# Four graph layers on one core: the edge half of the edge network moved into layer 1, products in PSUM, and a narrower layer 0

## What is computed

```python
x = _layernorm(x + _L0_gnn_ref(...))   # per type and head: softmax over the edges of a destination, weighted sum of x[src] @ W[type]
x = _layernorm(x + _L1_gnn_ref(...))   # three graph attention layers one after the other, 4 heads of 32
x = _layernorm(x + _L2_gnn_ref(...))   # an edge network, then a node network
x = _layernorm(x + _L3_gnn_ref(...))   # sum over the out-edges, one matrix, relu
```

```python
h = jnp.concatenate([x[row], edge_attr], axis=1)   # 128 + 128 columns
h = jax.nn.relu(h @ w1a + b1a)                     # 256 columns
h = jax.nn.relu(h @ w1b + b1b)                     # 256 columns
h = h @ w1c + b1c
summed = jax.ops.segment_sum(h, col, num_segments=n)
```

## Time and profile before

| what | us |
|---|---|
| median of 3 runs (10702.52 to 10762.04) | 10716.57 |
| the profiled execution | 10696.98 |
| its span, first to last instruction | 10695.3 |
| layer 0, 430 to 1885 | 1455 |
| layer 1, 1991 to 6545 | 4554 |
| edge network, 6605 to 8680 | 2075 |
| layer 3 scatter, 8900 to 10600 | 1700 |

### The profile page before, as it was taken

One profiled execution on the slowest core, in us unless ns is written; L12 is line 12 of the kernel. 1 busy time (PEld: TensorE's weight loads), 2 busy tenths in 40 slices (PEclk: granted clock), 3 DMA queues, 4 the chain that ended last, 5 costly groups with the idle time before them and its releaser, 6 DMA issues. The chain is left out here.

```text
span 10695.3 us, 86620 instructions
## 1 busy us (share of the span) xinstructions
PE 4520.8 (42%) x16860; PEld 2720.4 (25%) x16860; DVE 5556.2 (52%) x10266; ACT 2086.2 (20%) x4254; POOL 7165.4 (67%) x5805
## 2 busy tenths in 40 slices
PE   6388887211111200001000003888888885433332
PEld 5133333211110200001000001444444443333332
DVE  6399998644444344443444444555565544444443
ACT  1211111211111211112111112333333331000002
POOL 2466666488887688886888884555555526888885
PEclk8688888555555555555555556999999985555555
DMA  2433334322223222223222223333333313444445
GB/s 67 122 59 59 59 59 54 87 42 42 42 41 39 45 42 42 42 43 44 43 42 43 42 42 73 90 87 87 88 93 85 89 32 31 36 36 36 36 36 95
DMA packets 775295, 608.14 MB, mean 57 GB/s; under 512 B 441381, under 2 KB 661028, under 8 KB 774068
## 3 DMA queue, kind: packets, MB, share of 16 engines
q0 software_dynamic: 325728, 497.67, 26.0%
q1 hardware_dynamic: 449492, 109.67, 4.9%
HBM read 479.64 MB, written 127.21 MB: 57 GB/s over the span
## 5 line engine op out<-in xcount | busy, mean ns | idle before, releaser
L1640 POOL DMA_INDIRECT big<-table_layer,idx_L x2688 | 3528.8, 1313 | 952.3 <-issue 818.9
L2311 POOL DMA_INDIRECT sums_by_source<-msg,to x896 | 1420.4, 1585 | 286.9 <-issue 241.2
L1651 PE MATMUL own_ps_L<-of_tile_L,big 50*128 50x4 f32 x1344 | 313.1, 354 | 2694.4 <-DVE of_tile_L L1700 2694.4
L936 POOL DMA_INDIRECT big<-table_layer,idx_L x912 | 948.7, 1040 | 517.3 <-issue 299.0
L1710 DVE TENSOR_TENSOR z_L<-own_ps_L,big 128x64 f32<-128x64 f32 x168 | 43.9, 261 | 2034.5 <-DMA big<-table_layer,idx_L 2034.5
L1861 POOL DMA_INDIRECT big<-table_layer,from x900 | 861.1, 957 | 274.3 <-issue 274.3
L1651 PEld LDWEIGHTS own_ps_L<-of_tile_L,big 50*128 50x128 f32 x1344 | 298.6, 325 | 2712.2 <-DVE of_tile_L L1700 2704.7
L1911 PE MATMUL ps<-big,w 128*128 128x512 f32 x1792 | 829.6, 606 | 0.0
L1740 DVE TENSOR_TENSOR_SCAN big<-h 128x2244 f32<-128x2244 f32 x168 | 811.9, 4833 | 15.2
L999 PE MATMUL sums_L<-h,ident 128*128 128x512 f32 x1344 | 723.1, 688 | 169.6 <-issue 132.9
L1998 DVE TENSOR_REDUCE partial<-big 128x128 f32<-128x512 f32 x448 | 462.1, 1041 | 552.0 <-ACT big L1945 494.7
(11 more groups left out here) (411 smaller groups left out, 8962.7 us busy)
## 6 DMA issues: line engine op xcount, KB each, us to landing
big<-table_layer,idx_L POOLq DMA_INDIRECT x3600
table_layer<-xr SPq DMA_DIRECT2D x49, 298.0 KB
big<-table_layer,from POOLq DMA_INDIRECT x900
sums_by_source<-msg,to POOLq DMA_INDIRECT x896
sums_by_source<-big SPq DMA_DIRECT2D x4, 3200.0 KB
q<-sums_by_source SPq DMA_DIRECT2D x28, 448.0 KB, 6.2
own_L<-own_parts_layer SPq DMA_DIRECT2D x232, 40.0 KB
table_layer<-st_L SPq DMA_DIRECT2D x98, 66.0 KB
```

Source lines behind the costliest of these rows:

```text
L936: G.indirect_dma_start(out=g[b][:, u, s, :], out_offset=None, in_=table, in_offset=bass.IndirectOffsetOnAxis(ap=at, axis=0)).then_inc(gath ...
L1640: G.indirect_dma_start(out=ring[b][:, s, :], out_offset=None, in_=tab1_d[l], in_offset=bass.IndirectOffsetOnAxis(ap=idx[b][:, s:s + 1].bit ...
L1651: last = PE.matmul(own_ps[b % 2][:, c * B:(c + 1) * B], own1T[:, c * P:(c + 1) * P], of_tile[b % 2][:, :], start=True, stop=True)
L2311: G.indirect_dma_start(out=sum_d[s], out_offset=bass.IndirectOffsetOnAxis(ap=to[u][:, s:s + 1], axis=0), in_=msg[u][:, s, :], in_offset=No ...
```

## The change

Three things are changed, and small ones that they need.

1. **Layer 0.** `weigh` is one instruction of 2048 elements an item in place of four of 512. The weights (`wt`) lie in PSUM, two banks. The own part is picked by one copy and three predicated copies on a mask of the slot's type. The item sums use four PSUM banks in place of eight.
2. **Layer 1.** The products, the weights and the carried-in column lie in PSUM (`prod_ps`), handled in two halves of two heads: copy, copy, two products, scan of 1122 elements, twice a batch. The shrink factors stay in SBUF. In the first 13 turns of each of the three (52 of 56 batches), PE, ACT and SP also work through 5 or 6 chunks of 128 edges per batch: SP loads them in order, PE transposes them and multiplies by `w1a`'s edge half, ACT copies both results, SP stores 256 columns an edge to a new DRAM tensor `he_d`. Over the three layers this covers all edges. PE's small matmuls for a batch now stand one batch earlier.
3. **Edge network.** POOL gathers the window of four finished rows from `he_d` (4 KB a partition) and the four source rows. DVE adds the two in SBUF (1024 elements), PE transposes the sum (8), ACT applies the relu straight from PSUM, PE multiplies the second layer only. The edge transposes, the edge matmul, the mask and DVE's two copies and two additions are gone. Empty slots point at a source row lowered by 1e31, so that their first relu is 0; what they then add to the sums is a constant, taken off in the node network through a third row of `deg_d` and `brow`.

The core of the diff:

```diff
-                NB = 2 * B if T > 1 else B
+                NB = B
                 banks = [pb(f"sums_{tag}{v}", [P, 512], fp32, ph) for v in range(NB)]
...
-                        A.activation(sc[b][:, :, :, :], sc[b][:, :, :, :], ACT.Exp).then_inc(weighed, 1)
+                        A.activation(wt[b][:, :, :, :], sc[b][:, :, :, :], ACT.Exp).then_inc(weighed, 1)
...
-                            for u in range(B):
-                                V.tensor_tensor(zt[:, u, :, :].rearrange("p s (t w) -> p s t w", t=T),
...
+                            V.tensor_scalar(is_type[:, :, :], mask[b][:, :, :], 0.0, None, ALU.is_equal)
+                            V.tensor_copy(z[:, :, :, :], bc(ob[b][:, :, 0:ZW], 2, S))
                             dve.drain()
-
-                            V.tensor_reduce(z[:, :, :, :].rearrange("p u s w -> p (u s) w"),
...
+                            for t in range(1, T):
+                                V.copy_predicated(z[:, :, :, :].rearrange("p u s w -> p (u s) w"),
+                                                  bc(is_type[:, :, t], 2, ZW),
+                                                  bc(ob[b][:, :, t * ZW:(t + 1) * ZW], 2, S))
+                                dve.drain()
...
+                            last = V.tensor_tensor(
+                                prod[PROD[u]][:, :, :].rearrange("p s (t h c) -> p s t h c", t=T, h=H),
+                                bc(w.rearrange("p s (t h) -> p s t h", t=T), 4, C),
+                                bc(g[b][:, u, :, 0:D].rearrange("p s (h c) -> p s h c", h=H), 2, T), ALU.mult)
...
+                    prod_ps = pb(f"products_{tag}", [P, 3 * 512], fp32, ph)
+                    prod = prod_ps[:, 0:WIDE // 2].rearrange("p (a s) -> p a s", s=SLOTS + 1)
+                    wt = prod_ps[:, 1472:1472 + H * SLOTS].rearrange("p (h s) -> p h s", h=H)
...
+                            for f in range(2):
+                                rows = slice(f * half * (C + 1), (f + 1) * half * (C + 1))
+                                V.tensor_copy(prod[:, :, 0], tot[1 - b % 2][:, rows, SLOTS])
+                                V.tensor_copy(p4[:, :, C, 1:SLOTS + 1], wt[:, f * half:(f + 1) * half, :])
+                                for c in range(half):
+                                    hd = f * half + c
+                                    last = V.tensor_tensor(p4[:, c, 0:C, 1:SLOTS + 1], bc(wt[:, hd, :], 1, C),
...
+                        def hidden(i, b):
+                            k = i * NB + b
+                            for v in range(2):
+                                m = min(CHUNKS[b] - 4 * v, 4) * P
+                                act.wait_ge(e_turned, k * 2 + v + 5)
+                                A.activation(eT[:, 4 * v * P:4 * v * P + m], psE[:, 0:m], ACT.Copy).then_inc(eT_ok, 1)
...
+                        pool.wait_ge(joined, g + U - NH + 1)
...
+                        G.indirect_dma_start(out=gh[u % NH][:, :, :].rearrange("p s c -> p (s c)"), out_offset=None,
+                                             in_=he_flat, in_offset=bass.IndirectOffsetOnAxis(
...
+                        V.tensor_tensor(x_, x_, flat(gh[u % NH][:, :, :]), ALU.add).then_inc(joined, 1)
```

343 lines of the change are left out of this document (193 added, 150 removed).

## The result

The changed kernel took **10828.21 us** in the median of 5 runs (10809.93 to 10857.98), the kernel before 10716.57 beside it (5 runs too, in the range given above for 3): a ratio of 1.0112, 95% interval 1.0094 to 1.013. It is slower by 1.1%. I had forecast 9470 us, with 0.96 for faster and a range of 9190 to 9860. The forecast was wrong, by 1358 us and in its sign.

What follows compares the result with a forecast made beforehand. It took POOL's gather issue to bound layer 1, DVE layer 0 and PE the edge network. 10697 - 924 (layer 1) - 493 (edge network) + 171 (layer 0) + 10 (small things) = 9461, forecast 9470 us, range 9190 to 9860.

Steps and rivals of the forecast that it cites:

- What bounds layer 1: Layer 1: POOL's gather issue sets the pace; three gathers blocked beside DVE's products and scan cost 5.6 us a batch.
- The inference on the Trainium skill's page "SBUF — State Buffer": Layer 1 rival: gathers stay blocked, as descriptor generation is not stalled by tensor_tensor; nothing saved, 10385 us, chance 0.05.
- So the edge work is priced at nothing. Its cover is POOL's 20 us of gathers: Layer 1: edge work on PE, ACT and SP fits under POOL's gathers, ACT done at 19 to 21.5 us; cost nothing.
- the term of -924 us: Layer 1: with the gathers unblocked a batch falls from 26.1 to 20.6 us, saving 924 us over 168 batches.
- Another bound in layer 1: Layer 1 rival: ACT, with PE's edge work ahead of its keeps, bounds a batch at 22.3 us; 9750 us, chance 0.11.
- I subtracted 6.8 from 8.99: Edge network: POOL becomes the bound, an item falls from 8.99 to 6.8 us, saving 493 us over 225 items.
- the price of the new addition: Edge network: DVE's addition reads both inputs from SBUF and costs POOL's gathers 0.35 us an item.
- the mechanism: Layer 0: PE's fourth item waits for its bank, pauses 5.8 us, runs at half clock; DVE waits about 6 us.
- The predicated copies: Layer 0, DVE: three of 320 elements at 0.42 us each, 1.3 us in all; at twice that, 2.5.
- my 171: Layer 0: a batch grows from 24.9 to 27.9 us, losing 171 us over 57 batches.
- PSUM does not slow DVE: Layer 1 rival judged here: strided products and scan in PSUM slow DVE, kernel slower than before, 10771 us, chance 0.03.
- the rival said: Edge network rival: PE pauses, falls to half clock and needs about 8.3 us an item; 9799 us, chance 0.12.

Runs made afterwards that it cites:

- change_third: The changed kernel, unedited, on another chip: 9277.89 us, 0.908 of the kernel before.
- psum_products_alone: The kernel before with only layer 1's products and weights in PSUM, products and scan in two halves: 10275.08 us, 0.968 of the kernel before.
- twelve_small_third: psum_products_alone with 12 more semaphore increments on ACT per batch of layer 1: 9287.51 us, 0.909 of the kernel before.
- psum_alone_again: psum_products_alone, unedited, run once more on another chip: 10421.74 us, 0.973 of the kernel before.
- groups 1 and 3: Follow-up runs on two chips, each beside the kernel before, which took 10611.53 and 10712.04 us there.
- groups 2, 4 and 5: Follow-up runs on two other chips (the last two sets on the same one), beside the kernel before at 10235.79, 10222.68 and 10216.61 us.
- change_l0_keep_first: The changed kernel with ACT's first keep of a layer 0 batch put before the next batch's exponentials: 8942.01 us, 0.8752 of the kernel before.
- gathers_paced: psum_products_alone with a memset and a drain on POOL behind every second gather of layer 1: 12402.2 us, 1.212 of the kernel before.

## Why the prediction was wrong

**What bounds layer 1: right.** POOL's issue set the pace and three gathers a batch were blocked by DVE's products and scan. With PSUM operands a gather takes 0.952 us in the median; 18 of 2688 take over 1.4 us and none over 1.73, where 364 took over 1.4 and 178 over 3. Where nothing else intervenes the batch is 20.3 us (forecast 20.6). The inference on the Trainium skill's page "SBUF — State Buffer" (Who interferes with whom), that `tensor_tensor` with both inputs in SBUF does not stall descriptor generation, is contradicted: beside such products two gathers took 1.31 and 1.65 us, and with one operand of products and scans in PSUM POOL's gathers lost 954 us, most of it beside the scans.

**"So the edge work is priced at nothing. Its cover is POOL's 20 us of gathers": the step that failed, under one condition.** The overlap was wrong, and with it the 20.6 us a batch. The cover was the free time of ACT and SP under POOL's 20 us. In change_third the cover holds. In the run of the record it doesn't, and two parts of the loss can be told apart. The first has nothing to do with the edge work: once POOL is unblocked, on the chips with phases, ACT and SP don't keep up even with the `keep`s and index fetches that the kernel before had. psum_products_alone stands at 23.8 to 24.5 us a batch in its two runs, over 3 us above the forecast. The second is the edge work, 2.6 to 2.7 us more in the second and third tries and 4.5 to 5.3 in the first. POOL waits 1113 us more for indices than in change_third, and layer 1 takes 1148 us more (4495 for 3347). So the term of -924 us became +196. That it is ACT and SP that are late, and that the same code is not late on another chip, is shown; what makes them late stays open. My rival "Another bound in layer 1" named ACT with edge work ahead of the `keep`s, but at 22.3 us a batch it was too small, and it held the cause to be the amount of work.

**The edge network: the base was mis-sized.** I subtracted 6.8 from 8.99. But 8.99 held lost time already: the same code runs at 7.13 us an item in the groups without phases, bound there by PE, as a window over this stage in twelve_small_third shows (columns as in the earlier trace rows):

```profile
5620.00:7216.00 1596.00, 1581.49 (x7002) 872.79 (x7003) 1143.83 (x1965) 674.70 (x1094) 1068.16 (x1119) 1.00 0.44 112
```

PE is busy 1581 of 1596 us at full clock, where it was 1744 of 2075 at 0.92 in the record. Without phases the gain is 7.13 - 6.56 = 0.57 us, 128 us in all, not 493; with phases it was 8.99 - 8.15, 180 us from first to last start. The trace had told it: I read the mean of 225 starts and never asked why the median was 8.50 and some steps 19. What was right is the price of the new addition. Beside it five gathers take 0.37 us more an item (means of 1.029 and 1.031 us for 0.957 and 0.953; 0.26 without phases), forecast 0.35.

**Layer 0: the mechanism was right.** PE's pause was 5.44 us (forecast 5.8), the clock half, the passes 6.28 us (6.8), DVE's wait 6.21 (about 6), carry 0 came 11.6 us behind the end of weigh 3 (12.3), the batch 27.5 (27.9). The predicated copies were mis-sized: 0.52 us each (84.2 us for 162), between my two bounds of 0.42 and 0.84. The stage's 116 us stand against my 171; part of the rest is that I set 24.9 as the base where the mean was 25.4.

**Other rivals.** PSUM does not slow DVE: the products take 1.05 us each (1.00 before), the two half scans 2.49 each (4.83 in one). In the edge network of the changed kernel PE's clock was granted at 0.79 in the run of the record, with PE busy 1159 of 1810 us, and at 0.92 in change_third, with 1097 of 1460. So PE paused there too, as the rival said, but the clock held well enough for 6.56 us an item.

**The range.** It was made of costs inside the kernel. That the same kernel could run 5% apart on two chips, and that a change could be 9% faster on one and 1% slower on the other, was in none of its cases. 9277.89 us lies within it, by luck: the gain is 945 us from a base of 10223, and I had forecast 1236 from 10697. By terms, and with the record's 26.1 us for layer 1 before, since no other trace of that kernel was kept, layer 1 gives 168 x (26.1 - 20.3) = 974, the edge network 128, and layer 0 takes 57 x (27.3 - 24.9) = 137. That estimate adds up to 965.

## What to carry to other kernels

When an engine that held others back is freed, ask what rate the others then have to keep, in instructions and not only in busy time: a loop of five small instructions and one 0.43 us copy is cheap by its busy time and the first thing to suffer. Before subtracting from a stage's mean pace, look at the spread of its steps: in the kernel before, items of the edge network were 6 to 19 us apart, and 6 to 11 where there were no phases, so the mean of 8.99 had a second cause in it. And where one sum bank or buffer is freed by an engine that has other work in front of it, move that one release forward: here it was worth 336 us where there were no phases, and 0.6 us a batch where there were.

## What the runs showed of the hardware

**Phases of slow small instructions.** Counted over the register, move, branch and load instructions of ACT, SP and DVE that took 0.55 to 1.6 us, per 100 us:

| | layer 0 | layer 1, second try | edge network | layer 3 |
|---|---|---|---|---|
| before, record | 14.6 | 0.4 | 1.9 | 0.0 |
| changed, record | 10.7 | 22.8 | 4.8 | 0.0 |
| psum_alone_again | 17.2 | 30.5 | 2.0 | 0.0 |
| changed, change_third | 0.0 | 0.5 | 0.0 | 0.0 |

They occurred in groups 1 and 3 and in both kernels of the record (320 such instructions in the whole run of the kernel before, 908 to 1543 in the others), and hardly at all in groups 2, 4 and 5 (11 to 69). The code does not decide whether they occur: the changed kernel ran with them and without. It is not the load of instructions or packets as such: layer 1 of psum_alone_again has 4.4 instructions and 49 packets a us, and layer 3, free of phases, 8.7 and 95. In layer 1 of psum_alone_again 97% of 825 such instructions (of the second and third tries) lie within 5.0 us of the last start of a gather, and half of them over 22 us after the last break in POOL's stream of gathers (over 1.6 us from one start to the next). In before, where products and scan broke that stream 319 times in the same two tries, there are 12. So within layer 1 an unbroken stream of gathers goes with the phases, and the changed kernel's loss on such chips could be the other side of its gain, the blocked gathers having been the breaks. That is argued, not shown: both kernels with pauses ran where there were no phases, and layer 0 of the kernel before speaks against it. Its stream has 146 such breaks in 1397 us, and 209 slow instructions all the same, half of them within 3.5 us of a break.

**What stays open.** It is open whether the phases exist when nothing is recorded: each run here was timed and recorded at once. It is open what ACT does in the stretches of 8 to 9 us without any record. That they show as a fixed 0.70 us between records of two or three engines in turn would fit a path that the records share, and the counts above speak against a plain limit of its rate. The Trainium skill's page "NOTIFIC — the notification-queue block" (Constraints, capacities, measured rates) states that emitting an implicit record costs the engine no cycles; no run here shows whether that holds in a phase. Open too is what twelve more instructions cost in a phase, and how change_l0_keep_first stands there.

**A drain on POOL behind gathers** waits for them. In gathers_paced it is recorded with 3.6 to 3.7 us mostly, and the next gather starts 2.1 to 2.4 us later than it would.
